# Second message passing: per-edge factors on four scaled copies of the equality matrix

## The reference

```
w = ssp(edge_attr @ W_f1) @ W_f2 * (ssp(s0 @ W_s1) @ W_s2)
w1, w2, w3, w4 = split(w, 4)
x0e, x1e = split_irreps(x[edge_src])
out0 = w1 * x0e * sh0 + w4 * (x1e . sh1) / sqrt(3)
out1 = w2 * x0e * sh1 + w3 * x1e * sh0          # three components
out  = segment_sum(merge(out0, out1), edge_dst)
```

## Time and profile before

| | |
|---|---|
| time, median of 3 executions | 4578.88 us (4555.28 to 4579.88) |
| span of the profiled execution | 4670.9 us; the page gives no other time for this execution |
| TensorE busy | 4108.2 us, 88% |
| VectorE busy | 3416.2 us, 73% |
| GpSimd busy | 2813.0 us, 60% |
| ScalarE busy | 2670.2 us, 57% |
| stage of the second message passing | 2546 to 4448 us of the span |

### The profile page before, as it was taken

The page is one execution under the profiler, slowest core; times in us unless marked ns, Lnnn a source line. Parts: engine busy times, 40 slices in busy tenths (PEclk is TensorE's granted clock), DMA queues, the critical chain, the costliest instruction groups (busy, mean ns, idle before and its releaser), DMA issues. The chain is left out here.

```text
span 4670.9 us, 65873 instructions
## 1 busy us (share of the span) xinstructions
PE 4108.2 (88%) x16821; PEld 2295.3 (49%) x16821; DVE 3416.2 (73%) x9304; ACT 2670.2 (57%) x7162; POOL 2813.0 (60%) x2738
## 2 busy tenths in 40 slices
PE   7888888999999989979775889988889999999967
PEld 3344554555555545456454444444445555555543
DVE  8521226999999987667653888888888888888873
ACT  1111115888888871123254777777777777777720
POOL 1766664777777761013422777777777777777700
PEclk9988989999999999979887999999999999999978
DMA  4224115888888861257667999999999999988853
GB/s 178 89 96 138 37 37 179 255 257 256 252 256 255 253 214 59 83 190 232 194 210 248 223 223 225 221 228 225 223 230 222 222 224 222 224 218 217 181 167 134
DMA packets 368712, 910.65 MB, mean 195 GB/s; under 512 B 60879, under 2 KB 113086, under 8 KB 368089
## 3 DMA queue, kind: packets, MB, share of 16 engines
q0 software_dynamic: 209424, 663.87, 53.7%
q1 hardware_dynamic: 148287, 222.61, 14.4%
q10 hardware_dynamic: 10650, 20.19, 1.2%
HBM read 679.00 MB, written 227.92 MB: 194 GB/s over the span
## 5 line engine op out<-in xcount | busy, mean ns | idle before, releaser
L2126 POOL DMA_INDIRECT mid_acc<-m_out,m_il x416 | 688.4, 1655 | 149.9 <-issue 117.6
L2522 PE MATMUL m_pws<-m_w_s,m_hid 32*128 32x512 f32 x832 | 472.4, 650 | 138.9 <-DVE m_msg L2202 78.2
L2116 POOL DMA_INDIRECT m_drow<-mid_drow,m_ig x416 | 421.4, 1013 | 262.0 <-DMA m_ig<-in_gather_ix 111.8
L441 POOL DMA_INDIRECT mid_slots<-sort_rec,f_row x416 | 412.3, 991 | 264.8 <-issue 112.3
L807 POOL DMA_INDIRECT s_kv<-mid_kv_rows,keep_slot x440 | 425.9, 968 | 209.8 <-PE s_pm L1034 124.8
L1034 PE MATMUL s_pm<-s_kv,keep_free 128*128 128x260 f32 x1760 | 466.2, 388 | 47.5 <-ACT s_kv L951 37.5
L2530 PE MATMUL m_pm<-m_msg,m_same 128*128 128x512 f32 x832 | 491.4, 674 | 11.5 <-ACT m_out L2352 8.8
L2415 PEld LDWEIGHTS m_pip<-keep_ident,m_drow 128*128 128x128 f32 x2496 | 368.7, 204 | 246.3 <-issue 235.8
L2116 POOL DMA_INDIRECT m_srow<-mid_srow,m_ig x416 | 404.1, 971 | 126.9 <-issue 126.3
L2523 PE MATMUL m_pwf<-m_w_f,m_hid_f 32*128 32x512 f32 x832 | 476.7, 655 | 0.0
L1015 PE MATMUL s_pq<-queries_q,s_sameT 128*128 x880 | 467.8, 614 | 0.1
(11 more groups left out here) (396 smaller groups left out, 8619.1 us busy)
## 6 DMA issues: line engine op xcount, KB each, us to landing
mid_ys<-e_y SPq DMA_DIRECT2D x57, 256.0 KB
e_line<-in_src_lines POOLq DMA_DIRECT2D x52, 256.0 KB
m_line<-in_src_lines SPq DMA_DIRECT2D x104, 128.0 KB
m_xT<-mid_xhT SPq DMA_DIRECT2D x100, 128.0 KB
g_a<-mid_acc SPq DMA_DIRECT2D x50, 256.0 KB, 3.4
keep_w<-in_w SPq DMA_DIRECT2D x16, 512.0 KB
s_kv<-mid_kv_rows,keep_slot POOLq DMA_INDIRECT x440
mid_slots<-sort_rec,f_row POOLq DMA_INDIRECT x416
```

The costliest lines, as they stand in the source:

```text
L441: pool.indirect_dma_start(io["slots"], bass.IndirectOffsetOnAxis(ap=sort.row[:, e:e + 1], axis=0), sort.rec[:, e, :], None,).then_inc(s_pu ...
L2116: pool.indirect_dma_start(row, None, table, bass.IndirectOffsetOnAxis(ap=ig[:, n, t:t + 1], axis=0),).then_inc(s_g[t % S], 16)
L2126: pool.indirect_dma_start(io["acc1"][k % NACC], bass.IndirectOffsetOnAxis(ap=il[:, t:t + 1], axis=0), out[:, k % R, :], None, compute_op=A ...
L2522: pe.matmul(pws[k % 2][:], hid[lanes, par, :], w_s2[lanes, :], start=True, stop=True)
```

## The change

The factors sh0 and sh1 of an edge no longer multiply its features and messages. They multiply the rows of the equality matrix: ScalarE makes four scaled copies of `same`, one for each of the four factors (`scaled_same`), and TensorE's product with such a copy applies the factor to each edge as it sums. VectorE is left with the product of the two factors (as before) and two instructions that form eight plain products of 128 columns. In the order of `msg` these are w1 x0 (block 0), w3 times the three vector components (1 to 3), w4 times the three components (4 to 6) and w2 x0 (7). `sums` becomes four products into the same bank: one of 512 columns with the sh0 copy, and for each component c one of 256 columns with the sh1 copy, whose two blocks (w4 times component c, and w2 x0) go to the scalar part and to component c.

ScalarE's order changes: scaled(k+1) is last in its body, behind away_from and equals, and waits for the sums of two tiles before it (it took its buffer from `s_msg` before). TensorE's sums wait for the scaled copies in place of `same`. The next `equals` waits for scaled copies, not for sums. VectorE's `xs`, `xd`, `dot` and the step semaphore go.

```diff
@@ -2017,9 +2017,8 @@
         ipT, near = s.sb("ipT", [P, BW]), s.sb("near", [P, P])
         soft, hid = s.sb("soft", [P, P]), s.sb("hid", [P, 2, P])
         w = s.sb("w", [P, 2, D])
-        xs, xd = s.sb("xs", [P, 2, D]), s.sb("xd", [P, 2, 3 * P])
-        dot = s.sb("dot", [P, 2, P])
-        msg, same, out = s.sb("msg", [P, 2, D]), s.sb("same", [P, 2, B, P]), s.sb("out", [P, R, D])
+        msg, scaled_same = s.sb("msg", [P, 2, 8, P]), s.sb("scaled_same", [P, 2, 4, P])
+        same, out = s.sb("same", [P, 2, B, P]), s.sb("out", [P, R, D])
         pip, ph, pm, px = s.ps("pip", [P, D]), s.ps("ph", [P, P]), s.ps("pm", [P, D]), s.ps("px", [P, D])
         pws, pwf = ([s.ps(f"{n}{k}", [P, D]) for k in range(2)] for n in ("pws", "pwf"))
         s_w, s_pre = s.sem("weights"), s.sem("prepared")
@@ -2157,7 +2155,6 @@
                 w_dot = w_f2[:, 3 * P:D]
                 vec.tensor_scalar(w_dot, w_dot, 3.0 ** -0.5, None, ALU.mult).then_inc(s_pre, 1)
                 vec.wait_ge(s_pre, 2)
-                st = Steps(vec, s_st, DV)
                 def pair(b, k):
@@ -2173,34 +2170,23 @@
                     vec.scalar_tensor_tensor(hid[:, k // B % 2, :], ph[:], 0.0, soft[:], ALU.max, ALU.add).then_inc(s_hid, 1)
                 def message(b, k):
                     t, par = EU * b + k, k % 2
-                    st.begin(t)
-                    ws, msgs = pws[par][:], msg[:, par, :]
-                    x0 = srow[:, (EU * b + k) % S, 3 * P:4 * P]
-
-                    def three(x):
-                        return x.rearrange("p (c u) -> p c u", c=3)
-                    vec.wait_ge(s_xs, t + 1)
-                    st.did(vec.tensor_tensor(dot[:, par, :], xd[:, par, 0:P], xd[:, par, P:2 * P], ALU.add))
+                    ws = pws[par][:]
+                    x = srow[:, (EU * b + k) % S, 3 * P:SW].rearrange("p (c u) -> p c u", c=4)
                     vec.wait_ge(s_wf, t + 1)
                     vec.tensor_tensor(ws, ws, w[:, par, :], ALU.mult).then_inc(s_w2, 1)
-                    st.wait()
-                    st.did(vec.tensor_tensor(dot[:, par, :], dot[:, par, :], xd[:, par, 2 * P:3 * P], ALU.add))
                     vec.wait_ge(s_w2, t + 1)
                     need(vec, s_seg, t - 1)
-                    st.did(vec.tensor_tensor(three(msgs[:, P:D]), three(xs[:, par, P:D]),
-                                             ws[:, 2 * P:3 * P].unsqueeze(1).broadcast_to([P, 3, P]), ALU.mult))
-                    st.did(vec.tensor_tensor(ws[:, P:2 * P], x0, ws[:, P:2 * P], ALU.mult))
-                    st.did(vec.tensor_tensor(msgs[:, 0:P], xs[:, par, 0:P], ws[:, 0:P], ALU.mult))
-                    vec.wait_ge(s_st, DV * t + 2)
-                    st.did(vec.tensor_tensor(ws[:, 3 * P:D], dot[:, par, :], ws[:, 3 * P:D], ALU.mult))
-                    vec.wait_ge(s_st, DV * t + 4)
-                    for c in range(3):
-                        m = msgs[:, P * (c + 1):P * (c + 2)]
-                        vec.scalar_tensor_tensor(m, ws[:, P:2 * P], sh[:, t, 1 + c:2 + c], m, ALU.mult, ALU.add)
-                    st.wait()
-                    vec.tensor_tensor(msgs[:, 0:P], msgs[:, 0:P], ws[:, 3 * P:D], ALU.add).then_inc(s_msg, 1)
-                    st.end()
+                    fours = ws.rearrange("p (k u) -> p k u", k=4)
+                    scalars, vectors = msg[:, par, 0:8:7, :], msg[:, par, 1:7, :].rearrange("p (k c) u -> p k c u", k=2)
+                    vec.tensor_tensor(scalars, fours[:, 0:2, :], x[:, 0:1, :].broadcast_to([P, 2, P]), ALU.mult)
+                    vec.tensor_tensor(vectors, fours[:, 2:4, :].unsqueeze(2).broadcast_to([P, 2, 3, P]),
+                                      x[:, 1:4, :].unsqueeze(1).broadcast_to([P, 2, 3, P]), ALU.mult).then_inc(s_msg, 1)
                 def mixer(b, k):
@@ -2298,13 +2284,12 @@
                 def scaled(b, k):
                     t, par = EU * b + k, k % 2
-                    act.wait_ge(s_g[(EU * b + k) % S], 32 * ((EU * b + k) // S + 1))
-                    need(act, s_msg, t - 1)
-                    act.activation(xs[:, par, :], srow[:, (EU * b + k) % S, 3 * P:SW], ACT.Copy, scale=sh[:, t, 0:1])
-                    for c in range(3):
-                        ins = act.activation(xd[:, par, P * c:P * (c + 1)], srow[:, (EU * b + k) % S, P * (4 + c):P * (5 + c)], ACT.Copy,
-                                             scale=sh[:, t, 1 + c:2 + c])
-                    ins.then_inc(s_xs, 1)
+                    if k % B == 0:
+                        act.wait_ge(s_same, t // B + 1)
+                    need(act, s_seg, t - 1)
+                    for c in range(4):
+                        ins = act.activation(scaled_same[:, par, c, :], same[:, t // B % 2, k % B, :], ACT.Copy, scale=sh[:, t, c:c + 1])
+                    ins.then_inc(s_scaled, 1)
                 def factor(b, k):
@@ -2342,7 +2327,7 @@
                 def equals(q):
                     act.wait_ge(s_away, q + 1)
-                    need(act, s_seg, B * (q - 1))
+                    need(act, s_scaled, B * (q - 1))
                     act.activation(same[:, q % 2], away[:, q % 2], ACT.Relu, scale=-1.0, bias=1.0).then_inc(s_same, 1)
                 def rows(b, k):
@@ -2371,13 +2356,13 @@
                         need(act, s_ps, n)
                         act.activation(px[0:H, 0:P], px[0:H, 0:P], ACT.Copy, bias=1e-6).then_inc(s_zq, 1)
-                turn(0, 0)
-                soften(0, 0)
-                scaled(0, 0)
-                factor(0, 0)
                 for a in range(B):
                     away_from(0, a)
                 equals(0)
+                turn(0, 0)
+                soften(0, 0)
+                factor(0, 0)
+                scaled(0, 0)
                 def body(b):
                     for k in range(EU):
@@ -2389,13 +2374,14 @@
                         if k % B == 2 and (there := at(b, k + 2)):
                             soften(*there)
                         if there := at(b, k + 1):
-                            scaled(*there)
                             factor(*there)
                         q = 4 * b + k // B + 1
                         if q < ET // B:
                             away_from(q, k % B)
                             if k % B == B - 1:
                                 equals(q)
+                        if there := at(b, k + 1):
+                            scaled(*there)
                 for b in range(EB):
                     body(b)
                 rows(EB - 1, EU - 2)
@@ -2524,10 +2510,15 @@
                 def sums(b, k):
                     t = EU * b + k
-                    pe.wait_ge(s_same, 4 * b + k // B + 1)
+                    pe.wait_ge(s_scaled, t + 1)
                     pe.wait_ge(s_msg, t + 1)
                     need(pe, s_row, t)
-                    pe.matmul(pm[:], same[:, k // B % 2, k % B, :], msg[:, k % 2, :], start=True, stop=True).then_inc(s_seg, 1)
+                    sums, par = pm[:].rearrange("p (a u) -> p a u", a=4), k % 2
+                    pe.matmul(sums, scaled_same[:, par, 0, :], msg[:, par, 0:4, :], start=True, stop=False)
+                    for c in range(3):
+                        ins = pe.matmul(sums[:, 0:c + 2:c + 1, :], scaled_same[:, par, 1 + c, :], msg[:, par, 4 + c:8:3 - c, :],
+                                        start=False, stop=c == 2)
+                    ins.then_inc(s_seg, 1)
                 for k in range(B):
                     inner(0, k)
```

More of the change, by code:

```diff
@@ L2030, in edges1 @@
         s_add = [s.sem(f"added{k}") for k in range(R)]
-        s_prod, s_ip, s_ipT, s_h, s_soft, s_hid, s_wm, s_wf, s_w2, s_xs, s_st, s_away, s_same, s_msg, s_seg, s_row = (s.sem(n) for n in (
-            "pair_products", "inner", "innerT", "hidden_sums", "soft_steps", "hidden", "weight_products", "factors", "edge_weights", "scaled",
-            "steps", "distances", "same", "messages", "sums", "rows"))
+        s_prod, s_ip, s_ipT, s_h, s_soft, s_hid, s_wm, s_wf, s_w2, s_away, s_same, s_scaled, s_msg, s_seg, s_row = (s.sem(n) for n in (
+            "pair_products", "inner", "innerT", "hidden_sums", "soft_steps", "hidden", "weight_products", "factors", "edge_weights",
+            "distances", "same", "scaled_same", "messages", "sums", "rows"))
         s_mixw, s_half, s_extra, s_wp, s_heads = (s.sem(n) for n in ("mixer_weights", "half", "output_biases", "output_weights", "heads"))
@@ L2041, in edges1 @@
             "mixer_products", "queries", "keys", "values", "kv_sums", "kv"))
-        DV = 6
         PX = 4
```

## The result

The changed kernel takes 4916.5 us (median of four executions, 4911.0 to 4917.6) against 4573.2 us: 1.075 times as long, 95% interval 1.073 to 1.077. It is slower by 343 us. The forecast was 4995, with a range from 4900 to 5115.

A forecast was written before the change was run, and what follows sets the result against it. GpSimd's issues bound the kernel at 4.49 us a tile; TensorE would take over at 4.10 + 1.28 = 5.38, plus 0.10 waits and 0.05 clock: 5.53 x 416 + 20 = 2320 us, 418 more, 4995 us (8-in-10 range 4900 to 5115).

The forecast's parts named there:

- TensorE's stream before: TensorE's work per tile in the second message passing: 3.99 us in the key/value half, 4.21 in the query half, mean 4.10.
- The price of a narrow product: Three added 256-column products on TensorE cost 1.28 us a tile together; their separate blocks of 128 were taken as free.
- The tiles outside both halves: The 16 tiles outside the key/value and query halves were given TensorE's mean: 4.10 us before, 5.38 after.
- Waits around the bank: TensorE's next sums wait for ScalarE's scaling and copy-out of the one bank: loop 1.93 us, 0.1 us a tile.
- The clock: TensorE's granted clock, 0.96 over the stage and 0.50 after idle stretches, was to cost 0.05 us a tile.
- Fill and drain: Start and end of the second message passing stage: 20 us added to 416 tile periods.
- VectorE and ScalarE: VectorE saves 1.76 of 3.84 us a tile, ScalarE 0.39; neither sets the pace, so VectorE's saving is worth nothing by itself.
- The signs: Expected after: period 5.4 to 5.6 us, TensorE over 95% busy, sums 2.25 us, clock 0.97 or more, DMA below 0.8.
- TensorE has headroom: Rival, chance 0.03: TensorE is half idle, the addition fits under GpSimd's period, and the time stays 4579 us.
- VectorE was the limit: Rival, chance 0.03: VectorE set the pace before; its 1.76 us relief brings 4545 us if TensorE's addition is under 0.4.
- Cheaper than reckoned: Rival, chance 0.07: no ScalarE loop, no clock loss, some work overlapped on TensorE; 5.2 us a tile, 4860 us.
- Idleness stays: Rival, chance 0.08: TensorE's gaps remain and 1.28 us a tile comes on top of all, 532 us more, 5111 us.

The follow-up runs named there:

- the knee: Changed kernel with 0, 1, 2 or 4 instead of three 256-column products: 4540.3, 4565.9, 4732.4, 5089.9 us; added columns cost nearly nothing at first, their full length from two on.
- version without waits: Changed kernel with ScalarE's copy-out of the sums placed ahead of the scaling instead of behind it: 4870.8 us, 1.067 of before.
- GpSimd relieved: Kernel before with the indirect gather of receiver rows replaced by a plain load of 128 successive rows: 4458.1 us, 0.977 of before.

## Why the prediction was right

- *What bounded before.* GpSimd's issues at 4.49 us a tile: shown, by taking part of them away (106 us less) and by the knee. The DMA engines or VectorE as the bound are out by the same run.
- *TensorE's stream before.* 3.99 and 4.21 us a tile, with 1.28 added 5.27 and 5.49. The version without waits takes 5.241 us a tile in the key/value half and 5.492 in the query half. Both are met, to 0.03 us and less.
- *The price of a narrow product.* 0.427 us reckoned, 0.43 in the stages and 1.30/3 in the order of time. That separate blocks are free was taken without a row, and the kernel before with three more products bears it out.
- *The tiles outside both halves.* This term was mis-sized. I gave 16 tiles the mean, 5.38 us. In the version without waits the eight ahead of the mixer take 4.27 us each and the eight between its halves 4.75: 72 us where 86 were reckoned. The last seven periods, in which the stage runs out, are 4.57 us each, 12 us less than eight tiles of the query half. With 6 us in the key/value half that makes, but for rounding, the 31 us between 416 x 5.38 = 2238 and the measured 2207.
- *Waits around the bank.* 0.1 us a tile, 42 us, reckoned; 32.3 us of waits, 37.6 us in the stage. The loop is 2.00 us, the wait after a plain tile 0.21 to 0.28. Against the version without waits a tile is 0.107 us longer in the key/value half (5.348) and 0.064 in the query half (5.556). Right in place and size.
- *The clock.* 0.05 us a tile, 21 us, reckoned; it is 1.00 in every stretch, so nothing was lost. The gaps that had pulled it down to 0.50 are gone. The page "TensorE: Matmul & The Clock Gate" of the Trainium skill (Part 1: The HAM clock gate) has the throttled state as the default and activity releasing it; the trace agrees, with 1.00 where TensorE is busy for 98.5% of the stage.
- *Fill and drain.* 20 us on top of 416 periods; the stage from first to last copy-out has none.
- *The sum.* 31 + 4 (waits) + 21 + 20 = 76 us, which is what the measured stage (2244.3) lies under the reckoned one (2320). In the median the miss was 79 us. The path and the main term were right, but every smaller term erred upwards and none offset another. So the time came out at the low end of the range, and within 2 us of what the forecast held for its own lowest (4915). That lowest was no true bound either: it rests on 2238 us, and the version without waits takes 2207.
- *VectorE and ScalarE.* 0.42 and 0.95 us reckoned, 0.425 and 0.947 measured; 1.30 us for the copies, 1.28 measured. What VectorE saves was reckoned too high: 1.76 us of 3.84, which leaves 2.1, but it is busy for 2.75 us a tile (1144.36 us). Rows were added up one by one, though they overlap: 1248 of 345 ns would be 431 us, and cover 359.4. The time didn't depend on it. Their relief was worth nothing after the change, as put, though 25 us where TensorE adds nothing.
- *The signs.* Period, TensorE's share, the sums' 2.26 us, the wait of 0.3 us and the clock came as listed, and ScalarE is at 3.17 us. DMA is at 0.80, not below. GpSimd waits most for the hidden products, which the list doesn't name, and its old 4.49 us still shows between waits: that sign should have been put on its mean.
- *The rivals.* "TensorE has headroom" is out. The Trainium skill ("Perfetto Trace Analysis", Identifying the Most-Contended Engine) would judge that headroom by the weight loads, beside the share of peak arithmetic, which I didn't work out. The loads were 48% of the stage before and 61% in the version where TensorE never stops, while past the knee each added column showed in the time. Here the starts of the matmul rows told the stream of each half to within 0.03 us and the share of loads did not; the measurement decides. "VectorE was the limit" has its number nearly met by the run without narrow products (4540 against 4545, stage 1874 against 1868). It is out all the same: its condition was an addition under 0.4 us, which was 1.30, and with GpSimd relieved and VectorE's work left as it was the stage falls by 108 us. "Cheaper than reckoned" was right on the clock, but not in its 5.2 us a tile: even without the loop it is 5.317. "Idleness stays" is out: TensorE's idle time fell from 8% of the stage to 1.5%.

## What to carry to other kernels

Before moving work to another engine, read that engine's period from the starts of its instructions with the waits taken out, and set it beside the period of the engine that bounds: here TensorE's own 4.02 us (5.317 less 1.30) stood under a period of 4.569, so 0.55 us were free. The move cost 1.30, and the difference, 0.75, and 0.09 of waits for the bank came in the time. Work that is put on the matrix engine to spare a vector engine could not pay here, since the vector engine didn't bound. When two consumers wait for one event, put the one that frees a single buffer first: 38 us of the stage here, by moving two lines.

## What was not expected of the hardware

Nothing in the narrow products: three of 256 columns, on separate blocks of 128 in SBUF and in the bank, took 1.30 us where columns alone would take 1.28. What I had not expected is that a plain load issued by GpSimd takes it 1.08 us in the mean (211 loads in the stretch shown), hardly less than the 0.99 us of the indirect gather. Many of its rows begin before the scatter's row ends (at 3008.51 us, with a scatter from 3007.49 to 3009.11), so it seems to be this overlap, and the 0.30 us gap that falls away, that gives the time back: from that load to the next (3012.44) it is 3.93 us, where GpSimd's period was 4.49. Spans on GpSimd are rough in the profile, so the share of each is not shown.
